# Top-k attention: layer norm and the copy of output rows on ScalarE, division on GpSimd, unread products between scores and transposes

## The reference

```python
H, D, TOPK = 16, 8, 16
h = ln(x) * scale + shift                                  # scale and shift per sequence
q = (h @ w_q + b_q).reshape(B, L, H, D)
k, v = split((ctx @ w_kv + b_kv).reshape(B, 77, 2, H, D))
scores = einsum('bqhd,bkhd->bhqk', q, k) / sqrt(D)
top_s, top_i = top_k(scores, TOPK)                         # 16 of the 77 keys
attn = softmax(top_s)
o = einsum('bhqk,bhqkd->bqhd', attn, v[top_i]).reshape(B, L, C)
x = x + gate * (o @ w_co + b_co)
```

## Time and profile before

| | us |
|---|---|
| median of three runs | 3612.17 |
| lowest and highest | 3602.59, 3619.89 |
| the profiled execution, its own time | 3625.12 |
| its span, first to last instruction | 3623.3 |
| busy in the span: PE, DVE, ACT, POOL | 3124.1, 2815.1, 2170.7, 1200.7 |
| mean granted TensorE clock | 0.929 |

### The profile page before, as it was taken

The page is one execution under the profiler, slowest core; times in us unless marked ns, Lnnn a source line. Parts: engine busy times, 40 slices in busy tenths (PEclk is TensorE's granted clock), DMA queues, the critical chain, the costliest instruction groups (busy, mean ns, idle before and its releaser), DMA issues. The chain is left out here.

```text
span 3623.3 us, 94656 instructions
## 1 busy us (share of the span) xinstructions
PE 3124.1 (86%) x32127; PEld 2081.4 (57%) x32127; DVE 2815.1 (78%) x12664; ACT 2170.7 (60%) x5124; POOL 1200.7 (33%) x1534
## 2 busy tenths in 40 slices
PE   2999967777777769889999997889999998879999
PEld 2445534444444437656666665556666665558887
DVE  5677759999999978678887666968887765966665
ACT  1566645555555647557776565637776665646665
POOL 2000026666666656521112112531112211531221
PEclk9999978888889879989999898989999999979999
DMA  5000000000000000034444340024444431000000
GB/s 130 12 13 13 13 9 8 8 8 8 6 9 8 7 2 1 19 98 106 106 105 105 89 100 6 1 76 107 106 108 100 102 94 41 1 23 10 13 13 16
DMA packets 135427, 162.89 MB, mean 45 GB/s; under 512 B 40742, under 2 KB 85414, under 8 KB 134566
## 3 DMA queue, kind: packets, MB, share of 16 engines
q1 hardware_dynamic: 114182, 121.62, 13.5%
q0 software_dynamic: 12160, 26.04, 3.1%
q10 hardware_dynamic: 8608, 9.18, 1.0%
HBM read 13.81 MB, written 4.19 MB: 5 GB/s over the span
## 5 line engine op out<-in xcount | busy, mean ns | idle before, releaser
L1253 ACT ACTIVATE attn_pT<-attn_t 128x512 f32<-128x512 f32 (+1 forms) x1024 | 555.6, 596 | 333.9 <-PE attn_t L1510 333.8
L1370 DVE TENSOR_REDUCE attn_mx<-attn_s 128x4 f32<-128x512 f32 (+1 forms) x1024 | 549.7, 579 | 155.7 <-PE attn_s L1495 154.7
L636 ACT ACTIVATE topk_prob<-topk_s,topk_nmx 128x77 f32<-128x77 f32 x1024 | 248.3, 326 | 318.6 <-POOL topk_nmx L532 212.5
L1495 PEld LDWEIGHTS attn_s<-packed_keys,packed_queries 32*128 32x128 f32 x4096 | 280.7, 192 | 164.2 <-DVE attn_mx L1370 95.4
L1168 POOL DMA_DIRECT2D packed_queries<-attn_om x256 | 142.7, 558 | 655.7 <-ACT attn_om L1246 651.7
L1495 PE MATMUL attn_s<-packed_keys,packed_queries 32*128 32x128 f32 (+1 forms) x4096 | 346.0, 290 | 13.1 <-DVE attn_mx L1370 7.1
L1535 PE MATMUL attn_o<-attn_pT,attn_vp 128*18 128x128 f32 (+1 forms) x8192 | 331.0, 280 | 0.0
L538 POOL TENSOR_SCALAR topk_mask<-topk_work 128x308 f32<-128x308 f32 x256 | 252.9, 988 | 225.3 <-DVE topk_work L779 223.3
L927 PE MATMUL topk_t<-ident,topk_prob 128*77 128x128 f32 x1024 | 188.0, 314 | 136.7 <-POOL topk_prob L542 136.3
L1510 PE MATMUL attn_t<-packed_queries,packed_keys 32*128 32x128 f32 (+1 forms) x4096 | 302.8, 266 | 0.0
L927 PEld LDWEIGHTS topk_t<-ident,topk_prob 128*77 128x77 f32 x1024 | 140.8, 172 | 247.5 <-issue 141.1
(11 more groups left out here) (311 smaller groups left out, 7835.7 us busy)
## 6 DMA issues: line engine op xcount, KB each, us to landing
packed_queries<-attn_qT SPq DMA_DIRECT2D x720, 64.0 KB, 2.2
packed_keys<-attn_kT SPq DMA_DIRECT2D x384, 64.0 KB, 2.1
packed_queries<-attn_om POOLq DMA_DIRECT2D x256, 64.0 KB, 2.4
packed_queries<-zero_rows SPq DMA_DIRECT2D x120, 128.0 KB, 2.7
packed_keys<-attn_kT SPq DMA_DIRECT2D x384, 39.0 KB, 2.2
kbd<-window_kT SPq DMA_DIRECT2D x512, 8.0 KB
kbd<-topk_kT SPq DMA_DIRECT2D x512, 4.8 KB
weights<-in_weights ACTq DMA_DIRECT2D x1, 3524.5 KB, 14.5
```

Of the source, the lines that this page charges most:

```text
L636: last = nc.scalar.activation(prob[:, u % 4, h * keys:(h + 1) * keys], s_ps[:, u % 2, h * keys:(h + 1) * keys], ACT.Exp, scale=SCALE, bias ...
L1253: nc.scalar.activation(pT[0:keys, c % 2, h, :], t_ps[0:keys, h, :], ACT.Exp, scale=SCALE).then_inc(s_exp, 1)
L1370: nc.vector.tensor_reduce(mx[:, (c // 2) % 2, 2 * k + h, :], sc, AX.X, ALU.max).then_inc(s_max, 1)
L1495: last = nc.tensor.matmul(s_ps[:, h, k * KW:(k + 1) * KW], r.qp[32 * j:32 * j + 32, buf, k, b * T:(b + 1) * T], r.kp[32 * j:32 * j + 32, b ...
```

## The change

Only the phase of kind "topk" changes. On ScalarE: `nmx` is computed there (before: GpSimd), `ln_apply` writes `xn` as rstd * x + nmr (before: VectorE, subtract and multiply), and a new `rows_out` copies `r_ps`, values and row sums, into `orow` in SBUF. VectorE takes the reciprocals out of `orow`, one step later than before (`later` = 1), and GpSimd multiplies them onto the rows (`divide_rows`). GpSimd also computes `nmr` = -mean * rstd. `r_ps` is now given back to TensorE by `s_rows`. TensorE gets one product more, 128 x 128 by 128 x 512, in steps 2, 4, 6, 8, 10, 13, 14 and 15, behind `scores` and ahead of `transpose_probs`. It writes `l_ps`, which nobody reads, and so waits until `l_ps` has been read by whoever is to read it.

```diff
         mask = sb("mask", [T, 2, cols]) if topk else None
+        nmr = sb("nmr", [T, G]) if topk else None
...
-
-
-            c = lagged(u, NU + LO, first, units)
+        def sequence_hooks(u, first, units, later=0):
+
+
+            c = lagged(u, NU + LO + later, first, units)
             return c // NU if c is not None and c % NU == 0 else None
...
@@ -523,14 +527,14 @@
             def rstd_of(g):
                 pool.wait_ge(s_var, g + 1)
+                if topk:
+                    after(pool, s_xn, g)
                 nc.gpsimd.tensor_tensor(rstd[:, :], vareps[:, :], r.neg_half[:, :], ALU.pow).then_inc(s_rstd, 1)
-
-            def scale_maximum(i, u):
-                n = NS * i + u
-                after(pool, s_exp, n - 1)
-                after_alone(pool, s_top, n + 1)
-                nc.gpsimd.tensor_scalar(nmx[:, u % 2, :], top[:, u % 2, :, 0], -SCALE, None, ALU.mult
-                                        ).then_inc(s_dif, 1)
+                if topk:
+                    pool.wait_ge(s_rstd, g + 1)
+                    nc.gpsimd.tensor_tensor(nmr[:, :], mv[:, :, 0], rstd[:, :], ALU.mult).then_inc(s_nmr, 1)
+                    after_alone(pool, s_nmr, 2 * g + 1)
+                    nc.gpsimd.tensor_scalar(nmr[:, :], nmr[:, :], -1.0, None, ALU.mult).then_inc(s_nmr, 1)
             def pick(i, u):
...
+            def divide_rows(i, b):
+                m = G * i + b
+                if b % G == 0:
+                    after(pool, s_onps, i)
+                pool.wait_ge(s_rden, m + 1)
+                nc.gpsimd.tensor_tensor(on[:, b % G, :].rearrange("p (h d) -> p h d", d=D), orow[:, b % 2, :, 0:D],
+                                        rden[:, b % 2, :].rearrange("p (h a) -> p h a", a=1).broadcast_to([T, H, D]),
+                                        ALU.mult).then_inc(s_norm, 1)
+
             def prologue():
                 rstd_of(0)
                 rstd_of(1)
             def body(i, par, first, units, pre, ln):
-                for u in range(NS if units else 1):
-                    if topk and units:
-                        scale_maximum(i, u)
-                    c = lagged(u, 1, first, units)
+                for u in range(NS if units else PGT + 1):
+                    c = lagged(u, 1, first, units) if units or u == 0 else None
                     if topk and c is not None:
                         pick(i, c)
+                    b = sequence_hooks(u, first, units, 1) if topk else None
+                    if b is not None:
+                        divide_rows(i, b)
                     if ln and u == AGGR:
                         rstd_of(i + 2)
...
+            def ln_apply(g, bs=range(G)):
+                if bs[0] == 0:
+                    after(act, s_xT, g)
+                    act.wait_ge(s_nmr, 2 * g + 2)
+                for b in bs:
+                    last = nc.scalar.activation(xn[:, b:b + 1, :], r.x[:, bass.ds(G * g + b, 1), :], ACT.Identity,
+                                                scale=rstd[:, b:b + 1], bias=nmr[:, b:b + 1])
+                if bs[-1] == G - 1:
+                    last.then_inc(s_xn, 1)
+
+            def rows_out(i, b):
+                m = G * i + b
+                after(act, s_norm, m - 1)
+                act.wait_ge(s_otr, m + 1)
+                nc.scalar.copy(orow[:, b % 2], r_ps[:, :].rearrange("p (h c) -> p h c", c=32)[:, :, 0:VM]
+                               ).then_inc(s_rows, 1)
+
             def keys_out(g, par):
                 if split:
...
@@ -607,10 +638,14 @@
                                      ).then_inc(s_qT, 1)
             def prologue():
+                if topk:
+                    ln_apply(0)
                 modulate(0)
                 keys_out(0, 0)
                 queries_out(0, 0)
                 values_out(0, 0)
+                if topk:
+                    ln_apply(1)
             def body(i, par, first, units, pre, ln):
                 for u in range(NS if units else PGT + 1):
...
                     if units and topk:
                         n = NS * i + u
+                        act.wait_ge(s_top, n + 1)
+                        nc.scalar.activation(nmx[:, u % 2, :], top[:, u % 2, :, 0], ACT.Copy, scale=-SCALE
+                                             ).then_inc(s_dif, 1)
...
                         values_out(i + 1, 1 - par)
+                    b = sequence_hooks(u, first, units) if topk else None
+                    if b is not None:
+                        rows_out(i, b)
+                    if topk and ln and u in APPLY:
+                        ln_apply(i + 2, [b for b in range(G) if APPLY[b] == u])
...
                 after_alone(dve, s_stats, g + 1)
+                if topk:
+                    after_alone(dve, s_nmr, 2 * g)
...
+            def reciprocals(i, b):
+                m = G * i + b
+                after(dve, s_norm, m - 1)
+                dve.wait_ge(s_rows, m + 1)
+                nc.vector.reciprocal(rden[:, b % 2, :], orow[:, b % 2, :, D]).then_inc(s_rden, 1)
+
             def prologue():
...
+                if not topk:
+                    ln_apply(0)
                 low_keys(0)
                 low_queries(0)
                 ln_stats(1)
                 ln_variance(1)
-                ln_apply(1)
+                if not topk:
+                    ln_apply(1)
                 for w in range(NV):
                     values_out(0, 0, w)
...
                         ln_variance(i + 2)
-                    if ln and u in APPLY:
+                    if ln and u in APPLY and not topk:
                         ln_apply(i + 2, [b for b in range(G) if APPLY[b] == u])
-                    b = sequence_hooks(u, first, units)
-                    if b is not None:
+                    b = sequence_hooks(u, first, units, 1 if topk else 0)
+                    if b is not None and topk:
+                        reciprocals(i, b)
+                    elif b is not None:
                         normalise(i, b)
                     if not first and u == PGT:
...
+            def unread(i, u, first, pre):
+
+
+                if pre and u < 9:
+                    done = {2: s_hT, 4: s_kT, 6: s_qT, 8: s_v}[u]
+                    pe.wait_ge(done, i + 2)
+                elif u < 9:
+                    pe.wait_ge(s_pg, i - 1)
+                elif first:
+                    pe.wait_ge(s_v, 2)
+                else:
+                    pe.wait_ge(s_onT if u == 10 else s_pg, i)
+                nc.tensor.matmul(l_ps[:, :], r.W("m1_0", 0, T), r.W("m1_0", 0, GT), start=True, stop=True)
+
             def transpose_probs(i, c):
                 n = NS * i + c
...
                     after(pe, s_x, i if b > 0 else i - 1)
-                after(pe, s_norm, m)
+                after(pe, s_rows if topk else s_norm, m)
                 for g in range(NU):
...
                         scores(i, u, par)
+                    if topk and units and u in (2, 4, 6, 8, 10, 13, 14, 15):
+                        unread(i, u, first, pre)
                     c = lagged(u, LT, first, units)
                     if c is not None:
...
                                          ).then_inc(s_pjps, 1)
                     if not first and u == PGT:
-                        after(pe, s_norm, G * i + (1 if window else 2) if units else G * i)
+                        after(pe, s_rows if topk else s_norm,
+                              G * i + (1 if window else 2) if units else G * i)
```

More of the change, by code:

```diff
@@ L371, in attention_phase @@
         mask = sb("mask", [T, 2, cols]) if topk else None
+        nmr = sb("nmr", [T, G]) if topk else None
+        orow = sb("orow", [T, 2, H, VM]) if topk else None
         mx = sb("mx", [T, 2, HU])
@@ L393, in attention_phase @@
         s_mask = sem("mask")
+        s_nmr, s_rows = sem("nmr"), sem("rows")
         s_oT, s_otr, s_rden, s_norm = sem("oT"), sem("otr"), sem("rden"), sem("norm")
@@ L431, in lagged @@
             return c if (units if c >= 0 else not first) else None
-        def sequence_hooks(u, first, units):
-            c = lagged(u, NU + LO, first, units)
+        def sequence_hooks(u, first, units, later=0):
+            c = lagged(u, NU + LO + later, first, units)
             return c // NU if c is not None and c % NU == 0 else None
@@ L811, in prologue @@
                 ln_variance(0)
-                ln_apply(0)
+                if not topk:
+                    ln_apply(0)
                 low_keys(0)
```

## The result

The changed kernel takes 3686.5 us (median of 4 runs, 3685.1 to 3689.2) against 3607.4 for the kernel before on the same chip: a ratio of 1.0226 with a 95% interval of [1.0205, 1.0247]. It is slower by 2.3%, about 79 us. The profiled execution took 3685.1 us, its span is 3683.3 us, its mean clock 0.945 (before 0.929). From the first exp of the top-k phase to its last it takes 892.1 us (514.8 to 1406.9) where the kernel before takes 813.4, so the phase alone accounts for the loss: 78.7 us.

A forecast was written before the change was run, and what follows sets the result against it. DVE, 98% busy, was taken as the bound. New waiting of 71.7 us less 46.9 saved, about 2 more for prologue and tail, gave +27; the clock +52: 3612 + 79 = 3691 us, range 3618 to 3775.

The forecast's parts named there:

- The path: Products at u = 2, 4, 8, 10, 13 wait for ACT, delaying later scores: DVE waits over 70 us, most after 13.
- DVE's own work in a group: DVE, 16 steps: 50.6 us less 2.93 for `ln_apply`, `normalise` and idle time gives 47.7 us.
- 4.8 + 3.5 for the clock: DVE's new waiting per group: 4.78 us at full clock, plus 3.5 us for bursts at the lower clock level.
- the chain: DVE step u-1 through ACT's read, product, transposes, values and scores to DVE step u+1: late 4.78 us a group.
- price of a slow burst: PE behind a waiting product: at the lower level transposes, values, scores and product cost 2.2 us more.
- share of bursts that would be slow: PE's six bursts: 13 us if all slow, 7 at today's 28% share, half falling on bursts, so 3.5 us.
- ACT's work is small enough: ACT per group: 5.8 us of new work on 29.8, so 35.6 of 48 us, no bound by itself.
- The reciprocal out of SBUF: DVE's `normalise` becomes one reciprocal of 16 columns: 0.20 us instead of 0.52, saving 1.28 us a group.
- The idle 0.65 us goes too: DVE's present idle time per group, 0.65 us, was counted as saved in a new balance.
- GpSimd's new work is hidden: POOL gives away 16 `nmx` for four products and two small ones: less work than now, hidden.
- at most 10 us: Rival: unread products holding PE's clock at 2.4 GHz help by at most 10 us, already in the sum.
- faster: Rival: `l_ps` is read when PE asks, so DVE's saving of 47 us stands alone: 3565 us, chance 0.07.

The follow-up runs named there:

- the fastest kernel: The changed kernel with its products moved to steps 0, 3, 5, 7, 9, 11, 14 and 15, one each: 3551.7 us, ratio 0.9867 to the kernel before.
- three kernels with 0.85, 0.85 and 0.80: The changed kernel without its products, 3592.6 us; with six waits but no products, 3621.3 us; with only the product of step 13, 3650.8 us.

## Why the prediction was right

The forecast was 3691 us, 79 more than the 3612 of the kernel before; measured were 3686.5, 79 more than its 3607. The path was right: DVE's waits fall in the steps that were named, the largest behind step 13. The sizes agree less well than the sum. The measured lateness is that of the group shown under the result:

| | forecast | measured |
|---|---|---|
| DVE's own work in a group | 47.7 us | 47.9 |
| start of step 3 late (product u = 2) | 0.44 at full clock | 1.65, burst at lower level |
| step 5 (u = 4) | 0.54 | 0.39 |
| step 7 (u = 6) | 0 | 0, though PE waits 1.1 us |
| step 9 (u = 8) | 0.78 | 0.64 |
| step 11 (u = 10) | 1.30 at full clock | 2.69, burst at lower level |
| step 14 (u = 13) | 1.72 at full clock | 3.07, burst at lower level in its first part (4.2 in half of the groups) |
| sum of these rows | 4.8 + 3.5 for the clock = 8.3 | 8.4 |
| of it, what the lower clock adds | 3.5 | 4.3 |
| of it, the rest | 4.8 | 4.2 |
| group | 56.0 | 56.2 |

What the clock adds can be read from PE's rows, since two groups of the kernel after have the same wait ahead of step 2's burst, 2.41 us, and then different clocks. First the group shown, then an earlier one, whose stretch from 744.6 to 748.0 us has a granted clock of 1.00:

```profile
858.79 1.20 PE L989 MATMUL topk_l<-weights 128*128 128x512 f32 x2 [2.41 <-ACT topk_hT L586]
859.79 1.06 PE L996 MATMUL topk_t<-ident,topk_prob 128*77 128x128 f32 x4
860.78 0.62 PE L1018 MATMUL topk_o<-topk_pT,topk_vp 77*9 77x128 f32 x8
861.33 1.40 PE L972 MATMUL topk_s<-kbd,topk_qT 128*128 128x308 f32 x2
```

```profile
744.50 1.13 PE L989 MATMUL topk_l<-weights 128*128 128x512 f32 x2 [2.41 <-ACT topk_hT L586]
745.46 0.60 PE L996 MATMUL topk_t<-ident,topk_prob 128*77 128x128 f32 x4
745.99 0.41 PE L1018 MATMUL topk_o<-topk_pT,topk_vp 77*9 77x128 f32 x8
746.32 0.79 PE L972 MATMUL topk_s<-kbd,topk_qT 128*128 128x308 f32 x2
```

```profile
747.22 0.68 DVE L808 MAX8 topk_top<-topk_s 128x8 f32<-128x77 f32 x4 [0.33 <-PE topk_s L972]
```

From the product's start to the end of scores it is 3.94 us in the first and 2.61 in the second. The difference, 1.33 us, is what DVE is later (1.65 against 0.33). Measured the same way against rows at full clock, the burst of step 10 in the group shown took 1.55 us more and that of step 13 took 1.40 more; with the 1.33 of step 2 that is the 4.3 of the table. Other groups bear the rest out. Where the burst of step 10 ran at full clock (1.00 from 1112.0 to 1115.9 us), step 11 was 1.16 us late, and the forecast for full clock was 1.30:

```profile
1116.20 0.68 DVE L808 MAX8 topk_top<-topk_s 128x8 f32<-128x77 f32 x4 [1.16 <-PE topk_s L972]
```

So the chain was priced 0.6 us a group too high and the clock 0.8 too low, which is 9 and 12 us over 15 groups, and that the two cancel is luck. The 3.5 for the clock had its price of a slow burst right: 2.2 us without the output, and 2.1 measured in a group whose burst of step 13 was slow throughout (840.09 to 845.64 us). But no row stood behind the share of bursts that would be slow.

The cause is shown by runs: without the products the loss is gone, alone they make it, without their wait they do no harm, and with the wait met one step later they help. That ACT's work is small enough held: it is 71% busy in the fastest kernel (499.3 of 700 us), and its new instructions take 0.30 (`rows_out`), 0.22 (`nmx`) and 0.51 to 0.53 us (`ln_apply`, 0.38 to 0.40 to the next start). The forecast has `rows_out` at 0.35 and `ln_apply` at 0.30 but enters only 0.60 for the two ahead of `onT`; the trace has 0.56 there (885.00 to 885.56 us). The reciprocal out of SBUF, taken at 0.20, costs 0.16 to the next start (848.58 to 848.74).

What else was wrong stood beside the main line, in three places. "The idle 0.65 us goes too": without products it grew to 2.4 us. That GpSimd's new work is hidden: without products it puts off one pick a group by 0.5 us. And "at most 10 us" for products that keep the clock: true of the kernel before (3591 against 3602), but once the work has left VectorE they are worth 32 to 39 us (0.9974 without, 0.9884 and 0.9867 with). I had priced the clock by the waits in the trace of before, where DVE's longer steps covered PE's slow stretches. Moves and products each gave 0.2 to 0.3% alone, together 1.3%. For the rival case "faster", 3565 us was worked out from DVE's saving alone; it takes both halves to reach it.

## What to carry to other kernels

Filler work for an engine isn't free because the engine has time: ask what its wait stands in front of. Here 0.96 us in one step of sixteen cost some 60 us; eight of the same products where their buffer has long been read cost nothing (3600.6 us, a ratio of 1.0004). To find the place, add up the loop from the bound engine through the waited instruction and back to the bound engine, and compare it with that engine's own steps. And a cover that hides a slow engine is lost when the covering engine is relieved: price that before you price the relief.

## What the runs showed of the hardware that was not expected

- The mean clock and the time don't go together. The changed kernel has a higher clock in the phase than before (0.90 against 0.86) and is slower; of three kernels with 0.85, 0.85 and 0.80 the times go from 3593 to 3651 us. The mean doesn't tell at which level the bursts run for which DVE waits, and for one burst that made 1.3 us of lateness (1.65 against 0.33).
- The length of the pause ahead of a burst didn't settle its clock. After the same wait of 2.41 us a burst ran at 0.62 in one group and at 1.00 in another. After waits of 2.12 us it ran at 0.60 (886.3 to 890.0) and at 1.00 (1112.0 to 1115.9), and after waits of 1.1 to 1.4 us at 0.99 (862.5 to 886.0). After waits of 3.12 us it ran at 0.55 (897.7 to 901.0) and 0.50 (840.1 to 845.4). What decides between the levels these runs don't show.
- With hardly a wait left in the eight products (4.6 us in 710) the clock stayed at 1.00 for 700 us, though PE, by the trace, was busy for 85% of them only.
